# Order of the scores, the row maxima and what stands beside them in a step of TensorE

## The chip, the core and the metric

The kernel runs as one program on one core of a Trainium2 chip. The metric is the device time of an execution in microseconds; of the kernel before, three timed runs are given.

## What is computed

Eight sequences of 1024 tokens with 256 features go through two layers. Each layer normalises its input, and adds to it causal attention with 16 heads of 16 and a sparse expert network in which each token uses two of eight experts.

```
for x of 8 sequences:                        # (1024, 256)
    for layer in 0, 1:
        xn = layernorm(x)
        q, k, v = xn @ Wq.T, xn @ Wk.T, xn @ Wv.T
        o = softmax(causal(q k^T / 4)) v      # 16 heads of 16
        x = x + o @ Wo.T + experts(xn)
experts, layer 0: sum over 2 of 8 of score_e * (relu(xn @ W1[e] + b1[e]) @ W2[e] + b2[e])
experts, layer 1: sum over 2 of 8 of gate_e * (xn @ We[e] + be[e])
```

## The kernel before

A *run* is one sequence in one layer; there are 16. Runs are staggered on one long row of *steps*, written out by hand: each run has 48 steps of attention (a *unit*: one block of 128 keys for the four heads of a set, against up to 512 queries), and in the same steps TensorE does other runs' work. A table of step offsets (`XT`, `PROJ`, `VALUES`, `Y`, `OT`, `TURN`, ...) says when each of these is due. A *set* is four heads by 512 queries; it has 4 or 8 units. In the last four units of a set the scores get narrower (512, 384, 256, 128 columns), since queries ahead of the keys fall away.

All engines run their lists in order, and they meet through semaphores. `step(g)` of each engine writes the list. In TensorE's step, for j = 0 to 3, stand:

- `maxima` (M0 to M3, line 1160): bf16 scores with queries on the partitions, of another set, into the ring `pmx` of four banks. VectorE takes their row maxima (lines 875 and 879). In four steps of a group the products are 512 columns wide; in the steps on the diagonal they are 128, 256, 384 and 512 wide ("narrow maxima"), which is 32 of the 48 steps of a run;
- `scores` (S0 to S3, line 1147): bf16 scores of the unit with keys on the partitions, with the maxima folded in, into the ring `pst` of three banks. ScalarE makes the exponentials (line 722), one per head;
- beside the first member, `hidden` (H, line 1179), the first product of an expert tile of layer 0, which ScalarE reads at line 735;
- beside the third member, what the tables name: transposes of x (line 1216), `project` (line 1290, into `pmx`), `values` (line 1301), `project_output` (lines 1246 and 1249, into `pmx`);
- beside the fourth, `expert_out` (O, line 1194), which ScalarE copies at line 744.

Ahead of them a step may have `turn_tokens` (T, line 1168, read at line 727), and behind them the transposes of an ended set (line 1228), of the maxima (line 1222), and `attend` (A, line 1210) for the unit before. An expert tile starts every second step for 46 of 48 steps: in runs whose tiles are of layer 0, T and then H and then O stand in three steps that follow each other, so T and the O of the tile before share a step; with tiles of layer 1, T stands in odd steps and O in even ones. When a set ends, ScalarE copies its sums (`oraw`, line 751) between the first and the second exponential.

The rings give banks in TensorE's program order. The function `uses` counts them; `st` (line 1133) waits until the product three places earlier has been read, and `mx` until that four places earlier. GpSimd masks the block on the diagonal (line 621) once the fourth exponential is done, and then does its other work of the step, such as the last part of the split of a projection (line 627). VectorE splits the row maxima of a set in two instructions (lines 1042 and 1043).

Of the kernel before, what the change touches and what calls it, by code (L numbers as in the profile page):

```python
# [129 lines left out]
def unit(g):  # L130
    q, u = divmod(g, NU)
    return (q, u) if 0 <= q < NR else None
# [14 lines left out]
def tile_hidden(g):  # L147
    tile = tile_turned(g, 1)
    return tile if tile and layer(tile[0]) == 0 else None
# [32 lines left out]
def uses():  # L182

    mx, st = {}, {}
    for g in range(BEGIN, NR * NU + END - NU):
        if tile_turned(g):
            st["tokens", *tile_turned(g)] = len(st)
        work = maxima_at(g)
        turns = at_step(g, TURN)
        for j in range(GH):  # L190
            for q, n, k in work[j:j + 1]:
                mx["max", q, n, k] = len(mx)
            if j == 2:
                for (c, k), q in at_step(g, XT):
                    st["xT", q, c, k] = len(st)
                for (c, n), q in at_step(g, PROJ):
                    mx["proj", q, c, n] = len(mx)
                for t, q in at_step(g, VALUES):
                    st["v", q, t] = len(st)
                for b, q in at_step(g, Y):  # L200
                    mx["y", q, b] = len(mx)
            if j == 3 and tile_out(g):
                st["out", *tile_out(g)] = len(st)
            if unit(g):
                st["unit", *unit(g), j] = len(st)
            if j == 0 and tile_hidden(g):
                st["hidden", *tile_hidden(g)] = len(st)
        for q, n in set_ended(g):
            mx["set", q, n] = len(mx)
        for n, q in turns:  # L210
            mx["turn", q, n] = len(mx)
        for c, q in at_step(g, OT):
            for k in range(KD):
                st["oT", q, c, k] = len(st)
        for _, q in at_step(g, [GATE_ROWS]):
            mx["pos", q] = len(mx)
            mx["gateT", q] = len(mx)
        for _, q in at_step(g, [INVERSE]):
            mx["rows", q] = len(mx)
    return mx, st  # L220


MX, ST = uses()


def attention_moe_kernel(nc, A, out):
    ctx = ExitStack()
    with ctx:
# [462 lines left out]
        def _(act):  # L691
# [72 lines left out]
            def middle_parts(q, c, n):  # L764
                act.wait_ge(mx_read, mx_done("proj", q, c, n))
                act.activation(parts[:, n // 2, n % 2, 1], rest[:, n % 2], ACT.Copy).then_inc(mid_ready, 1)  # L766
# [20 lines left out]
            def step(g):  # L787
# [9 lines left out]
                    exponentials(*unit(g), 1)  # L797
                for (c, n), q in at_step(g - 1, PROJ):
                    middle_parts(q, c, n)
                for (c, k), q in at_step(g, XT):  # L800
                    take_x(q, c, k)
                for (c, n), q in at_step(g, PROJ):
# [1 line left out]
                for t, q in at_step(g, VALUES):  # L804
                    take_values(q, t)
                if unit(g):
                    exponentials(*unit(g), 2)
                if tile_out(g):
                    take_result(*tile_out(g))
                if unit(g):  # L810
                    exponentials(*unit(g), 3)
                for _, q in at_step(g, [GATES + 1]):
                    if layer(q) == 1:
                        act.wait_ge(logits_ready, q // 4 * 2 + q % 2 + 1)
# [311 lines left out]
        def _(pe):  # L1126
# [184 lines left out]
            def step(g):  # L1311
                work = maxima_at(g)
                if tile_turned(g):
                    turn_tokens(*tile_turned(g))
                for j in range(GH):
                    for piece in work[j:j + 1]:
                        maxima(*piece)
                    if j == 2:
# [7 lines left out]
                            project_output(q, b)  # L1326
                    if j == 3 and tile_out(g):
                        expert_out(*tile_out(g))
                    if unit(g):
                        scores(*unit(g), j)  # L1330
                    if j == 0 and tile_hidden(g):
                        hidden(*tile_hidden(g))
                for q, n in set_ended(g):
                    turn_set(q, n)
                for n, q in at_step(g, TURN):
# [58 lines left out]
```

## Time and profile before

| | us |
|---|---|
| three timed runs | 3098.23, 3103.86, 3106.82 (median 3103.86) |
| profiled execution | 3109.94 |
| its span from the first to the last instruction | 3108.2 |
| TensorE matmuls, weight loads busy | 2990.0, 1585.0 |
| VectorE, ScalarE, GpSimd busy | 2420.6, 1973.1, 1191.5 |

Matmuls overlap, so that the busy time of TensorE says little of what it could still take; the distance between two starts says how long one holds the next. In the rows, "k_first" and "k_second" are the two halves of the keys, `probs` the exponentials. A row of a timeline has the start in us from the span's start, the duration in us, the engine, the line, the operation, and what it writes and reads.

### The profile page before, as it was taken

Reading aid. Unit: us, or ns where it says so; the run is one execution under the profiler, and the core shown is the slowest. Engines: PE = TensorE matmul, PEld = TensorE weight load, DVE = VectorE, ACT = ScalarE, POOL = GpSimd, SP = SyncE. Lnnn points to the kernel's source line nnn. Section 1 sums busy time; section 2 is a strip of 40 time slices with the busy share of each in tenths; the row PEclk is TensorE's granted clock in tenths of the full one; section 3 lists DMA queues with packets and bytes.
Section 4 is the critical chain, followed back from the end, with each engine's and each line's share of the span. In section 5 each row is a group of like instructions: output and inputs, shape, how many; then the busy total and the mean of one; then the engine's idle time right before and its main releaser. Section 6 shows DMA issues by size and latency. Waiting matters only on the chain.

```text
span 3108.2 us, 62739 instructions
## 1 busy us (share of the span) xinstructions
PE 2990.0 (96%) x19312; PEld 1585.0 (51%) x19312; DVE 2420.6 (78%) x7517; ACT 1973.1 (63%) x4954; POOL 1191.5 (38%) x1424
## 2 busy tenths in 40 slices
PE   5899999999999999999999999999999999999998
PEld 3555555445455554545445555454545555545453
DVE  6677788887877778888777787878887777787884
ACT  2566666666666666666666666666666666666665
POOL 3225235252432524435252352534425244252533
PEclk8999999999999999999999999999999999999999
DMA  5677445364554645446364464635537455453542
GB/s 141 184 180 209 137 138 157 116 184 133 165 186 128 179 135 161 150 113 182 118 200 148 146 179 140 173 108 148 177 108 214 139 171 170 128 162 110 162 141 69
DMA packets 276876, 473.27 MB, mean 152 GB/s; under 512 B 52960, under 2 KB 185792, under 8 KB 274496
## 3 DMA queue, kind: packets, MB, share of 16 engines
q1 hardware_dynamic: 236928, 379.48, 40.5%
q0 software_dynamic: 29952, 81.83, 9.8%
q10 hardware_dynamic: 9664, 7.93, 0.9%
q8 instruction: 159, 2.61, 0.3%
q14 instruction: 173, 1.42, 0.2%
HBM read 344.19 MB, written 130.03 MB: 153 GB/s over the span
## 4 chain that ended last, share of the span: by engine, by line
PE 78%; DVE 10%; issue 4%; DMA 4%; ACT 3%; SPq 1%; POOL 1%; ACTq 0%; DVEq 0%; POOLq 0%
PE po L1210 16%; PE pmx L1160 14%; PE pst L1147 13%; PE pst L1194 9%; PE pmx L1290 5%; PE pst L1179 5%; PE pst L1301 4%; DVE pmx L879 3%; PE pmx L1249 3%; PE pst L1168 3%; DMA wt<-w_tiles 2%; PE pmx L1228 2%; PE pst L1216 2%; DVE rmax L875 1%; ACT probs L722 1%
## 5 line engine op out<-in xcount | busy, mean ns | idle before, releaser
L722 ACT ACTIVATE probs<-pst 128x512 f32<-128x512 f32 (+3 forms) x3072 | 1402.5, 497 | 413.6 <-PE pst L1147 409.6
L621 POOL TENSOR_SCALAR_AFFINE_SELECT probs<-probs 128x512 f32<-128x512 f32 x512 | 326.2, 637 | 1473.6 <-ACT probs L722 1472.5
L875 DVE TENSOR_REDUCE rmax<-pmx 128x1 f32<-128x512 f32 x1024 | 671.0, 682 | 133.0 <-PE pmx L1160 126.5
L1147 PE MATMUL pst<-qs,k_first 98*128 98x512 bf16 (+3 forms) x2048 | 689.2, 342 | 8.7 <-ACT probs L722 4.3
L1160 PE MATMUL pmx<-k_first,qs 96*128 96x512 bf16 (+2 forms) x2048 | 669.5, 343 | 14.3 <-DVE rmax L879 5.7
L879 DVE CUSTOM_DVE_ANT_0 pmx<-pmx,mask,rmax 128x128 f32<-128x128 f32 (+3 forms) x1024 | 534.5, 555 | 164.2 <-PE pmx L1160 154.3
L1210 PE MATMUL po<-probs,v 128*32 128x512 f32 (+3 forms) x6144 | 656.0, 499 | 4.2 <-POOL probs L621 4.2
L879 DVE CUSTOM_DVE_ANT_0 pmx<-pmx,mask 128x128 f32<-128x128 f32 (+3 forms) x1024 | 483.3, 509 | 138.0 <-PE pmx L1160 136.8
L594 POOL DMA_INDIRECT xg<-xn_rows,rows_of x368 | 357.9, 973 | 95.7 <-issue 50.8
L1160 PEld LDWEIGHTS pmx<-k_first,qs 96*128 96x128 bf16 x2048 | 198.8, 98 | 348.5 <-issue 123.7
L1160 PE MATMUL pmx<-k_second,qs 96*128 96x128 bf16 (+3 forms) x1024 | 304.9, 302 | 17.4 <-DVE otok L1016 8.7
L1147 PE MATMUL pst<-qs,k_second 98*128 98x512 bf16 (+3 forms) x1024 | 300.4, 301 | 3.0 <-ACT probs L722 2.2
L608 POOL DMA_INDIRECT yk<-y_slots,slot x256 | 245.1, 957 | 127.4 <-DVE x L1036 48.1
L1147 PEld LDWEIGHTS pst<-qs,k_first 98*128 98x128 bf16 x2048 | 199.6, 98 | 178.0 <-ACT probs L722 50.9
L879 DVE DVE_READ_ACCUMULATOR2_ANT rmax<- 128x1 f32 x2048 | 287.4, 140 | 0.0
L744 ACT ACTIVATE ys<-pst 128x256 f32<-128x256 f32 x368 | 142.9, 388 | 179.5 <-PE pst L1194 135.8
L1290 PE MATMUL pmx<-xnT,wqk 128*128 128x512 f32 x512 | 248.0, 607 | 7.4 <-DVE rmax L875 6.6
L1210 PEld LDWEIGHTS po<-probs,v 128*32 128x32 f32 x6144 | 121.2, 108 | 219.8 <-issue 171.9
L627 POOL TENSOR_TENSOR parts<-rest,parts 128x512 bf16<-128x512 f32 x128 | 148.8, 1163 | 191.9 <-ACT parts L766 191.9
L727 ACT ACTIVATE xgT<-pst 128x256 f32<-128x256 f32 x368 | 142.6, 387 | 118.8 <-PE pst L1168 116.3
L1179 PE MATMUL pst<-xgT,wt 128*128 128x128 f32 x1472 | 198.9, 279 | 19.7 <-DMA wt<-in_b 11.6
L1179 PEld LDWEIGHTS pst<-xgT,wt 128*128 128x128 f32 x1472 | 190.1, 194 | 36.2 <-DMA wt<-in_b 13.1
(143 smaller groups left out, 3514.3 us busy)
## 6 DMA issues: line engine op xcount, KB each, us to landing
wt<-w_tiles SPq DMA_DIRECT2D x161, 513.0 KB
qk_parts<-parts SPq DMA_DIRECT2D x256, 192.0 KB
y_slots<-ys SPq DMA_DIRECT2D x368, 128.0 KB
wt<-w_tiles SPq DMA_DIRECT2D x184, 256.0 KB
qs<-qk_parts SPq DMA_DIRECT2D x128, 192.0 KB
xn_rows<-xn SPq DMA_DIRECT2D x16, 1024.0 KB, 6.1
qs<-qk_parts SPq DMA_DIRECT2D x128, 128.0 KB
k_first<-qk_parts SPq DMA_DIRECT2D x64, 192.0 KB, 3.8
```

The costliest lines, as they stand in the source:

```text
L594: pool.indirect_dma_start(out=xg[:, m % XRING], out_offset=None, in_=xn_dram[q % 2], in_offset=bass.IndirectOffsetOnAxis(ap=rows_of[:, q % ...
L608: pool.indirect_dma_start(out=yk[:, m % GRING], out_offset=None, in_=y_dram[q % 2], in_offset=bass.IndirectOffsetOnAxis(ap=slot[:, q % 2, ...
L621: pool.affine_select(out=tri, in_=tri, compare_op=ALU.is_ge, fill=0.0, base=0, pattern=[[0, GH], [1, P]], channel_multiplier=-1).then_inc( ...
L722: act.activation(probs[:, u % 2, j, 0:w], ps[:, 0:w], ACT.Exp, scale=DH ** -0.5).then_inc(st_read, 1)
L875: dve.tensor_reduce(rmax0[:, col:col + 1], src, AX_X, ALU.max).then_inc(mx_read, 1)
L879: dve.tensor_tensor_reduce(out=src, in0=src, in1=mask[:, BANK - (b - a):BANK], op0=ALU.add, op1=ALU.max, scale=1.0, scalar=rmax0[:, col:co ...
L1147: pe.matmul(ps[:, 0:w], keys[0:SROWS, j, k % HT * P:(k % HT + 1) * P], qs[0:SROWS, set_no(q, n) % QRING, j, a:a + w], start=True, stop=Tru ...
L1160: pe.matmul(bk[:, 0:b - a], qs[0:STACK, set_no(q, n) % QRING, j, t % HT * P:(t % HT + 1) * P], keys[0:STACK, j, 0:b - a], start=True, stop ...
L1179: mm = pe.matmul(ps[:, j * P:(j + 1) * P], wt[:, m % WRING, a:a + P], xgT[:, m % 2, k], start=(k == 0), stop=(k == KD - 1))
L1194: mm = pe.matmul(ps[:, 0:D], src[:, m % 2, k], wt[:, m % WRING, a:a + D], start=(k == 0), stop=(k == KD - 1))
L1210: mm = pe.matmul(po[HS * j:HS * (j + 1), BANK - w:BANK], v[:, q % 2, k, col:col + HS], probs[:, u % 2, j, 0:w], start=(k == 0), stop=(u in ...
L1290: mm = pe.matmul(ps[:], wqk[l][:, m, k, tile * P:(tile + 1) * P], xnT[:, k, c * BANK:(c + 1) * BANK], start=(k == 0), stop=(k == KD - 1))
```

## The change

In TensorE's step the pair of a member is turned round: the scores (and, at the first member, `hidden`) come first, then the piece of maxima, then what stands beside the member. So the products beside the third member stand behind its scores, and `expert_out` stands behind all four scores. The counts of the rings follow. ScalarE takes the third exponential ahead of x, the projection's high part and the values, and the fourth ahead of the copy of `expert_out`. VectorE, GpSimd and the DMA lists are the same.

```diff
@@ uses(), and likewise step(g) of TensorE
         for j in range(GH):
+            if unit(g):
+                st["unit", *unit(g), j] = len(st)
+            if j == 0 and tile_hidden(g):
+                st["hidden", *tile_hidden(g)] = len(st)
             for q, n, k in work[j:j + 1]:
                 mx["max", q, n, k] = len(mx)
             if j == 2:
...
             if j == 3 and tile_out(g):
                 st["out", *tile_out(g)] = len(st)
-            if unit(g):
-                st["unit", *unit(g), j] = len(st)
-            if j == 0 and tile_hidden(g):
-                st["hidden", *tile_hidden(g)] = len(st)
@@ step(g) of ScalarE
                     middle_parts(q, c, n)
+                if unit(g):
+                    exponentials(*unit(g), 2)
                 for (c, k), q in at_step(g, XT):
                     take_x(q, c, k)
...
                 if unit(g):
-                    exponentials(*unit(g), 2)
+                    exponentials(*unit(g), 3)
                 if tile_out(g):
                     take_result(*tile_out(g))
-                if unit(g):
-                    exponentials(*unit(g), 3)
```

TensorE's list in a step with O (unit 34 of a run, expert tiles of layer 1), before:

```order
L1160 MATMUL pmx<-k_second,qs 128x128
L1147 MATMUL pst<-qs,k_first 128x512
L1160 MATMUL pmx<-k_second,qs 128x256
L1147 MATMUL pst<-qs,k_first 128x512
L1160 MATMUL pmx<-k_second,qs 128x384
L1147 MATMUL pst<-qs,k_first 128x512
L1160 MATMUL pmx<-k_second,qs 128x512
L1194 MATMUL pst<-wt,xgT 128x256 x2
L1147 MATMUL pst<-qs,k_first 128x512
L1210 MATMUL po<-probs,v 32x512 x4
```

and after the change:

```order
L1147 MATMUL pst<-qs,k_first 128x512
L1160 MATMUL pmx<-k_second,qs 128x128
L1147 MATMUL pst<-qs,k_first 128x512
L1160 MATMUL pmx<-k_second,qs 128x256
L1147 MATMUL pst<-qs,k_first 128x512
L1160 MATMUL pmx<-k_second,qs 128x384
L1147 MATMUL pst<-qs,k_first 128x512
L1160 MATMUL pmx<-k_second,qs 128x512
L1194 MATMUL pst<-wt,xgT 128x256 x2
L1210 MATMUL po<-probs,v 32x512 x4
```

L1147 are the scores, L1160 the maxima, L1194 is O and L1210 A. The four scores now stand with one M between two of them, and O stands ahead of A, behind the last M.

TensorE's list in a step with H (unit 34, tiles of layer 0), before:

```order
L1160 MATMUL pmx<-k_second,qs 128x128
L1147 MATMUL pst<-qs,k_first 128x512
L1179 MATMUL pst<-xgT,wt 128x128 x4
L1160 MATMUL pmx<-k_second,qs 128x256
L1147 MATMUL pst<-qs,k_first 128x512
L1160 MATMUL pmx<-k_second,qs 128x384
L1147 MATMUL pst<-qs,k_first 128x512
L1160 MATMUL pmx<-k_second,qs 128x512
L1147 MATMUL pst<-qs,k_first 128x512
L1210 MATMUL po<-probs,v 32x512 x4
```

and after:

```order
L1147 MATMUL pst<-qs,k_first 128x512
L1179 MATMUL pst<-xgT,wt 128x128 x4
L1160 MATMUL pmx<-k_second,qs 128x128
L1147 MATMUL pst<-qs,k_first 128x512
L1160 MATMUL pmx<-k_second,qs 128x256
L1147 MATMUL pst<-qs,k_first 128x512
L1160 MATMUL pmx<-k_second,qs 128x384
L1147 MATMUL pst<-qs,k_first 128x512
L1160 MATMUL pmx<-k_second,qs 128x512
L1210 MATMUL po<-probs,v 32x512 x4
```

H (L1179) keeps its place behind the first scores, but the first M now stands behind H; the last M stands behind the last scores.

ScalarE's list around the copy of an ended set's sums (L751), in a step with T, O and a projection's middle part (L766), before:

```order
L727 ACTIVATE xgT<-pst 128x256
L722 ACTIVATE probs<-pst 128x512
L751 ACTIVATE oraw<-po 128x512
L722 ACTIVATE probs<-pst 128x512
L766 ACTIVATE parts<-rest 128x512
L722 ACTIVATE probs<-pst 128x512
L744 ACTIVATE ys<-pst 128x256
```

and after:

```order
L727 ACTIVATE xgT<-pst 128x256
L722 ACTIVATE probs<-pst 128x512
L751 ACTIVATE oraw<-po 128x512
L722 ACTIVATE probs<-pst 128x512
L766 ACTIVATE parts<-rest 128x512
L722 ACTIVATE probs<-pst 128x512 x2
L744 ACTIVATE ys<-pst 128x256
```

The copy of O (L744) has moved from ahead of the fourth exponential to behind it.

## Rows read from the trace of the kernel before

**Rows 1.** The page: busy time, and the clock in 40 slices.

```profile
PE 2990.0 (96%) x19312; PEld 1585.0 (51%) x19312; DVE 2420.6 (78%) x7517; ACT 1973.1 (63%) x4954; POOL 1191.5 (38%) x1424
...
PEclk8999999999999999999999999999999999999999
```

**Rows 2.** Groups by form, TensorE: busy us, mean ns, idle us, releasers.

```profile
L1147 PE MATMUL pst<-qs,k_first 98*128 98x512 bf16 x1280 | 480.0, 382 | 4.6 <-ACT probs L722 3.4 <-ACT attn L785 0.3
```

**Rows 3.** The view of waits: us in total, times, longest us.

```profile
PEld pmx L1160 <- DVE rmax L879: 118.4, 200, 1.2
...
PEld pst L1147 <- ACT probs L722: 65.2, 181, 0.9
...
PEld pst L1194 <- ACT probs L722: 25.2, 73, 0.9
```

**Rows 4.** Timeline, TensorE, step with O: start, us, instruction.

```profile
1560.21 0.22 PE L1160 MATMUL pmx<-k_second,qs 96*128 96x128 bf16 x1
1560.27 0.38 PE L1147 MATMUL pst<-qs,k_first 98*128 98x512 bf16 x1
1560.48 0.27 PE L1160 MATMUL pmx<-k_second,qs 96*128 96x256 bf16 x1
...
1561.48 1.10 PE L1194 MATMUL pst<-wt,xgT 128*128 128x256 f32 x4
1562.42 0.38 PE L1147 MATMUL pst<-qs,k_first 98*128 98x512 bf16 x1
1562.73 0.64 PE L1210 MATMUL po<-probs,v 128*32 128x512 f32 x4
```

**Rows 5.** Timeline, ScalarE, same step.

```profile
1560.74 0.60 ACT L722 ACTIVATE probs<-pst 128x512 f32<-128x512 f32 x1 [0.61 <-PE pst L1147]
1561.24 0.59 ACT L722 ACTIVATE probs<-pst 128x512 f32<-128x512 f32 x1
```

**Rows 6.** Timeline, TensorE, step with T.

```profile
1563.73 0.44 PE L1168 MATMUL pst<-ident,xg 128*128 128x128 f32 x2
...
1565.52 0.64 PE L1210 MATMUL po<-probs,v 128*32 128x512 f32 x4
```

**Rows 7.** Timeline, ScalarE, same step.

```profile
1564.20 0.38 ACT L727 ACTIVATE xgT<-pst 128x256 f32<-128x256 f32 x1 [0.65 <-PE pst L1168]
1564.54 0.60 ACT L722 ACTIVATE probs<-pst 128x512 f32<-128x512 f32 x1
1565.04 0.59 ACT L722 ACTIVATE probs<-pst 128x512 f32<-128x512 f32 x1
```

**Rows 8.** Timeline, TensorE, step with H.

```profile
1198.56 0.22 PE L1160 MATMUL pmx<-k_second,qs 96*128 96x128 bf16 x1
...
1198.84 1.06 PE L1179 MATMUL pst<-xgT,wt 128*128 128x128 f32 x8
...
1200.99 0.64 PE L1210 MATMUL po<-probs,v 128*32 128x512 f32 x4
```

**Rows 9.** Timeline, ScalarE, same step.

```profile
1199.99 0.62 ACT L735 ACTIVATE hT<-pst,wt 128x128 f32<-128x128 f32 x2 [0.30 <-PE pst L1179]
```

**Rows 10.** Timeline, TensorE, step with T, O and a set's end.

```profile
1193.82 0.44 PE L1168 MATMUL pst<-ident,xg 128*128 128x128 f32 x2
...
1195.46 1.10 PE L1194 MATMUL pst<-wt,hT 128*128 128x256 f32 x4
...
1196.62 0.60 PE L1228 MATMUL pmx<-ident,oraw 128*128 128x128 f32 x4
```

**Rows 11.** Timeline, ScalarE, same step, second exponential.

```profile
1195.64 0.66 ACT L722 ACTIVATE probs<-pst 128x512 f32<-128x512 f32 x1
```

**Rows 12.** VectorE instructions of line 1043: ns min/median/max.

```profile
L1043 DVE SCALAR_TENSOR_TENSOR mparts<-rmax,mparts x128: 174/175/1719, 61.6 to 3061.5; 128x16 bf16<-128x16 f32 x128
```

**Rows 13.** Timeline, GpSimd, beside a long one of line 1043.

```profile
1052.82 1.15 POOL L627 TENSOR_TENSOR parts<-rest,parts 128x512 bf16<-128x512 f32 x1
```

**Rows 14.** Timeline, VectorE, the long one.

```profile
1052.30 1.71 DVE L1043 SCALAR_TENSOR_TENSOR mparts<-rmax,mparts 128x16 bf16<-128x16 f32 x1
```

More of the change, by code:

```diff
@@ L1315, in step @@
                 for j in range(GH):
+                    if unit(g):
+                        scores(*unit(g), j)
+                    if j == 0 and tile_hidden(g):
+                        hidden(*tile_hidden(g))
                     for piece in work[j:j + 1]:
@@ L1328, in step @@
                         expert_out(*tile_out(g))
[L1329 to L1332, printed above, removed]
                 for q, n in set_ended(g):
```

## The prediction

> **What bounds the kernel now.** I began with the page: the matmul side of TensorE is busy for 2990.0 of 3108.2 us and the clock row stands at 9 nearly everywhere, so every stage hangs on TensorE at its 2.4 GHz level [rows 1]. But busy time here is the sum of overlapping durations. By form, a 512-column score product lasts 382 ns [rows 2], while in a step two neighbours start 0.21 us apart (1560.27 and 1560.48 [rows 4]). So I read starts, not durations, and asked where one start lies further behind the last than the columns explain. The view of waits names the candidates [rows 3]: weight loads of the row maxima held by VectorE for 118.4 us, those of the scores held by ScalarE's exponentials for 65.2 us, those of the experts' last product for 25.2 us. (A weight load is where TensorE waits; not all of it reaches the matmuls.) TensorE takes its instructions in program order, so any such wait delays all that follows. The change moves the work that lies between such waits.
>
> The ring behind the score waits is `pst`, three banks. Write S0 to S3 for the scores of a step, M0 to M3 for the maxima, T for the token transposes, H for `hidden`, O for `expert_out`, A for `attend`. T, H, O, the scores, and also the transposes of x and the values (X below) go through the ring in program order, and each needs the product three places earlier to have been read by ScalarE. M, `project` and the output projection use the other ring, `pmx`, that VectorE empties.
>
> **The change, part by part.** No product is added or removed. Per step, each M moves behind the S of its number, H moves ahead of M0, products beside the third member move behind S2, and O moves behind S3 and M3. Total streaming is the same; fixed gaps at A should be too. What changes is the distance between scores, and whom O waits for.
>
> *Step with O and no T.* Before: S0 starts at 1560.27, O at 1561.48, S3 at 1562.42, A at 1562.73, 2.52 us after the step's M0 [rows 4]. ScalarE ends the first exponential at 60.74 + 0.60 = 61.34, which is S0 + 1.07, and the second at 61.83, S0 + 1.56 [rows 5]. O stood 0.14 behind the first one's end, since its fp32 weight load comes after the wait. I use 0.05 for a score after such an end and 0.14 for O. After: S0 at 0, M0 0.21, S1 0.27, M1 0.48, S2 0.59, M2 0.81, and S3 would be due at 0.97 (narrow maxima stream 0.05, 0.11, 0.16 and 0.21 us). Its ring place is S0's, free at 1.12. Then M3, and O would start at 1.55 but now needs S1's place: 1.56 + 0.14 = 1.70. O to the next product took 0.94, A stands 0.09 behind: 2.73. Loss 0.21 us.
>
> *Step with T, no O.* Before 1.79 us from T to A [rows 6]. Tokens are read at 64.59, T + 0.86; exponentials end at T + 1.41 and T + 1.90 [rows 7]. After: S2, due at T + 0.87, needs the tokens' place, 0.91; S3, due at 1.29, needs S0's, 1.46; M3 to 1.89; A at 1.98. Loss 0.19.
>
> *Step with T and O.* Before, from the same rows, O at 1.41 + 0.14 = 1.55, A at 1.55 + 0.94 + 0.31 = 2.80. After, O at 1.90 + 0.14 = 2.04, A at 3.07. Loss 0.27.
>
> *Step with H.* Before 2.43 from M0 to A [rows 8]. `hT` is read at 1199.99 + 0.62 = 1200.61, H + 1.77 [rows 9]. H now starts at S0 + 0.21, S3 needs its place: 0.21 + 1.77 + 0.05 = 2.03 (due at 1.84), M3, A at 2.03 + 0.21 + 0.21 + 0.09 = 2.54. Loss 0.11, with roundings 0.12.
>
> *Step with T, O and the end of a set.* ScalarE copies `oraw` between the first and the second exponential, so the second ends at 1195.64 + 0.66 = 1196.30, T + 2.48 [rows 11]. Before, O needed only the first and ran under this copy, from T + 1.64; the transposes of the set start at T + 2.80 [rows 10]. After, O waits until 2.62 and the set until 3.56. Loss 0.76; I take 0.7, since the earlier fourth score of the step before lightens ScalarE's backlog.
>
> Where the maxima of a step are all 512 wide, S3 falls due at 1.29 (no T) and 1.56 (T), behind 1.12 and 1.46: no loss, except where the scores are 128 wide (S2 due at 0.81 against 0.91: 0.1). With `project` or the output projection behind S2, S3 is late anyway: no loss, and its exponential no longer queues behind the copy of the projection. Where x's transposes or the values stand there, they now wait for the first exponential themselves: about 0.16.
>
> *Counts.* A run has 48 steps; in half of the 16 runs the expert tiles are of layer 0 (with H), in half of layer 1. Steps of one pair of runs with narrow maxima: O alone with wide scores 4 x 0.21, one more 0.1; T alone 2 x 0.19 and, with narrower scores, 6 x 0.15; T and O 2 x 0.27 and 5 x 0.15; H 6 x 0.12; set with T and O 3 x 0.7, and one held by VectorE anyway 0.15; set with T 3 x 0.16; X beside the third member 12 x 0.16; wide maxima under 128-wide scores 6 x 0.1. Sum 9.5 us, times 8: 76 us. The 0.15 and 0.16 are estimates from the four steps above with shorter exponentials.
>
> *What comes back.* M waits: each S now stands ahead of the M that waits, but the M that starts VectorE's chain is later by an S as well. I take nothing. VectorE's queue, though, is filled by blocked instructions: the second part of the maxima's split takes 175 ns in the median and up to 1719 ns [rows 12], and a long one ends at 1052.30 + 1.71 = 1054.01, just behind GpSimd's subtraction, 1052.82 + 1.15 = 1053.97 [rows 13, 14]. That GpSimd work stands behind the causal mask, which waits for the fourth exponential; S3 now comes ahead of O and the chain moves forward by up to 1 us, out of the split's way. The bound: one long split in each of 16 runs, 1719 - 175 ns each, 25 us of VectorE, of which TensorE can get back only what it waits for afterwards. I take 10; the ends are 0 and 25.
>
> The Trainium skill (SBUF — State Buffer, Who interferes with whom) says that a VectorE instruction with two SBUF inputs blocks against a GpSimd instruction that reads SBUF, whichever came first holding the ports to its end. The split has two SBUF inputs, and the two ends agree within 0.04 us. By the rule the chain only has to shift, and may as well fall on another VectorE instruction; by the row I count the relief.
>
> Sum: 3109.94 (the profiled execution) + 76 - 10 = 3176. The median of the three runs, 3103.86, lies 6 lower: 3170 us, +2.1%.
>
> The Trainium skill (Perfetto Trace Analysis, Optimization Strategy) says that a gap that repeats on the engine that should be saturated can mean too few buffers for the next tile. Here the repeat is O's 0.14 us behind an exponential. By the rule, spacing ring users apart helps, and the change does the reverse.
>
> **The rivals.** *Absorbed.* TensorE's new waits fall where it would have waited for VectorE a step later; the 118.4 us of held weight loads speak for it, against it that in the steps worked out VectorE has no part. If nine tenths vanish: +8, about 3112. *Faster.* The place is the first steps behind a projection. If the whole bound of 25 us reaches TensorE and ScalarE's shorter queue there gives 5 more, 30 us come back; it decides if ScalarE's freed places are seen some 0.2 us earlier than I read them, which takes the losses away in all but the set steps (3 x 0.7 x 8 = 17). Then 3104 + 17 - 30 = 3091. Against it: O stood 0.14 behind the exponential, so the places are felt. *Deeper.* In H steps M0 now comes behind H, so VectorE idles under H and gets four maxima in a row; if that adds 0.3 us to each of the 8 x 23 steps with H, +55: 3225.
>
> **How the numbers follow.** Forecast 0.62, absorbed 0.13, faster 0.11, deeper 0.14. Its own range is 3145 to 3190 (losses a third smaller, or no relief). For 8 in 10 I reach down half way to the absorbed case and up part of the way to the deeper one: 3118 to 3198. What a measurement of this kernel can tell from no change is 0.3%, 9 us. Absorbed straddles that: 0.06 of it same, 0.07 slower; slower in all 0.83, same 0.06, faster 0.11.
>
> **What would show it.** After, in a step with O, A should start 2.7 us after S0, with O close behind the second exponential; T to A 1.98; the set step's O at T + 2.6. Waits of L1147 and L1194 for L722 should at least double, those of L1160 for VectorE stay or shrink, and the long splits at step 0 be gone. I am wrong if the fourth score starts 0.97 after the first in such a step, or if DVE waits grow instead.

## The result, and the profile after

| | us |
|---|---|
| before, four runs beside the changed kernel | 3105.34 (3098.23 to 3107.44) |
| changed, four runs | 3187.64 (3184.88 to 3188.56) |
| ratio | 1.0262, interval 1.0245 to 1.0280 |
| span of the profiled execution | 3108.2 before, 3186.8 after |

The change makes the kernel 82 us slower; between the two profiled spans it is 78.6. The page of the kernel after, with its busy times and the clock:

```profile
PE 3050.2 (96%) x19312; PEld 1547.8 (49%) x19312; DVE 2417.3 (76%) x7517; ACT 1962.4 (62%) x4954; POOL 1193.2 (37%) x1424
...
PEclk8999999999999999999999999999999999999999
```

The counts are those of [rows 1], and so is the clock row: TensorE is granted its 2.4 GHz level nearly all the time in both (the granted clock is 0.991 of full speed in the mean before and 0.993 after; 0.002 of 3108 us is 6 us, an estimate of the most that this gave the changed kernel). Its busy share is 96% as before, with 2.6% more time. The share says nothing here; a matmul that waits under the end of the one before it looks busy. The view of waits after, total us, times, longest:

```profile
PEld pst L1147 <- ACT probs L722: 199.8, 401, 1.0
...
PEld pst L1147 <- ACT ys L744: 97.3, 116, 0.8
POOL yk L608 <- DVE x L1036: 82.5, 63, 3.5
PEld pst L1147 <- ACT xgT L727: 81.9, 310, 0.4
...
PEld pmx L1160 <- DVE rmax L879: 64.7, 134, 1.0
...
PEld pst L1194 <- ACT probs L722: 47.4, 88, 0.9
```

Against [rows 3], the scores' waits for the exponentials tripled (65.2 to 199.8 us), those of O nearly doubled (25.2 to 47.4), and those of the maxima for VectorE halved (118.4 to 64.7). TensorE has traded waits for VectorE for waits for ScalarE. (A wait in this view need not cost time. The 97.3 us of the scores for `ys`, which had no such row before, stand behind A: in unit 26 S0's weight load starts 0.99 us behind A's start, where M0's did before.) The steps show what the waits are worth.

*Step with O, no T.* TensorE's timeline, the same step as [rows 4]:

```profile
1597.68 0.38 PE L1147 MATMUL pst<-qs,k_first 98*128 98x512 bf16 x1
...
1598.80 0.39 PE L1147 MATMUL pst<-qs,k_first 98*128 98x512 bf16 x1
1599.03 0.38 PE L1160 MATMUL pmx<-k_second,qs 96*128 96x512 bf16 x1
1599.38 1.10 PE L1194 MATMUL pst<-wt,xgT 128*128 128x256 f32 x4
1600.41 0.64 PE L1210 MATMUL po<-probs,v 128*32 128x512 f32 x4
```

S3 starts 1.12 us after S0, O 1.70, A 2.73: the three numbers worked out before, to the hundredth. Before, the step took 2.52, so it costs 0.21.

*Step with T.* TensorE, the same step as [rows 6]: T, S2, S3, A. Then ScalarE's reading of the tokens and its first exponentials:

```profile
1601.41 0.44 PE L1168 MATMUL pst<-ident,xg 128*128 128x128 f32 x2
...
1602.32 0.39 PE L1147 MATMUL pst<-qs,k_first 98*128 98x512 bf16 x1
...
1602.81 0.39 PE L1147 MATMUL pst<-qs,k_first 98*128 98x512 bf16 x1
...
1603.35 0.64 PE L1210 MATMUL po<-probs,v 128*32 128x512 f32 x4
```

```profile
1601.88 0.38 ACT L727 ACTIVATE xgT<-pst 128x256 f32<-128x256 f32 x1 [0.92 <-PE pst L1168]
1602.16 1.57 ACT L722 ACTIVATE probs<-pst 128x512 f32<-128x512 f32 x3
```

S2 starts at T + 0.91 as worked out, but S3 at T + 1.40 (I had 1.46) and A at T + 1.94 (1.98). ScalarE's first exponential starts at T + 0.75; in [rows 7] it was T + 0.81. The reason stands in the order of the instructions: S0 used to follow M0 and now comes ahead of it, 0.06 us earlier. I had carried the old exponential times over unchanged.

*Step with H.* TensorE, the same step as [rows 8]: S0, H, S3, A; then ScalarE's `hT`:

```profile
1227.88 0.38 PE L1147 MATMUL pst<-qs,k_first 98*128 98x512 bf16 x1
1228.10 1.05 PE L1179 MATMUL pst<-xgT,wt 128*128 128x128 f32 x8
...
1229.93 0.39 PE L1147 MATMUL pst<-qs,k_first 98*128 98x512 bf16 x1
...
1230.47 0.64 PE L1210 MATMUL po<-probs,v 128*32 128x512 f32 x4
```

```profile
1229.25 0.62 ACT L735 ACTIVATE hT<-pst,wt 128x128 f32<-128x128 f32 x2 [0.30 <-PE pst L1179]
```

`hT` is read at 1229.87, H + 1.77 as in [rows 9]; S3 follows 0.06 later and A 0.54 after that. The step takes 2.59 instead of 2.43.

*Step with T, O and the end of a set.* TensorE, the same step as [rows 10], then ScalarE, where the copy of `oraw` (L751) stands ahead of the second exponential as in [rows 11]:

```profile
1222.53 0.44 PE L1168 MATMUL pst<-ident,xg 128*128 128x128 f32 x2
...
1225.00 1.10 PE L1194 MATMUL pst<-wt,hT 128*128 128x256 f32 x4 [0.46 <-ACT probs L722]
1225.94 0.60 PE L1228 MATMUL pmx<-ident,oraw 128*128 128x128 f32 x4
```

```profile
1223.77 0.59 ACT L751 ACTIVATE oraw<-po 128x512 f32<-128x512 f32 x1
1224.25 0.61 ACT L722 ACTIVATE probs<-pst 128x512 f32<-128x512 f32 x1
```

The second exponential ends at 1224.86, T + 2.33; O starts at T + 2.47 and the set at T + 3.41, against T + 1.64 and T + 2.80 before.

Taken over the whole program, from the start of one A to that of the next in each of the 768 steps, the difference of the two traces falls on the kinds of step as follows (sums over the 16 runs):

| kind of step | worked out | measured |
|---|---|---|
| O alone, narrow maxima | 6.7 | 6.8 |
| T alone | 3.0 | 2.4 |
| T alone, narrower scores | 7.2 | 6.2 |
| T and O | 4.3 | 3.2 |
| T and O, narrower scores | 6.0 | 5.4 |
| H | 5.8 | 7.3 |
| set with T and O, three steps | 16.8 | 13.4 |
| set with T and O, unit 25 and the narrow one | 1.2 | 6.7 |
| set with T | 3.8 | -1.0 |
| x's transposes or values beside the third member | 15.4 | 17.5 |
| 128-wide scores under wide maxima | 4.8 | 4.7 |
| sum of these | 75.0 | 72.7 |
| units 0 and 40, which gained | 0 | -9.4 |
| units 4, 5, 31 and 32, which lost | 0 | 13.4 |
| unit 26 | 0 | -3.1 |
| all other steps | 0 | 5.2 |
| relief of VectorE's queue, somewhere | -10 | none found |

(The prediction's 76 has one more O step at 0.1, and roundings; the measured column sums to 78.8 up to roundings, the spans differ by 78.6.) So most losses stand where they were placed, and what stayed away is the relief. The two sums, 75.0 and 72.7, agree better than their rows, which miss by -4.8 to +5.5 us: that part of the agreement is luck.

One more wait differs between the two traces, and the prediction has no term for it. In steps with H, TensorE waits until the expert's weights have landed; what L1179 waited for, us in total and times, first before, then after:

```profile
  DMA wt<-w_tiles: 20.4, 21
```

```profile
  DMA wt<-w_tiles: 9.6, 17
```

The view adds the idle time of the weight loads to that of the matmuls, so that the time won is about half of the difference, some 5 us. In the traces of the twelve versions the figure is anything from 4.6 to 31.2. The waits fall mostly in units 0, 4 and 40 with tiles of layer 0, and one trace of each kernel doesn't show whether their shrinking here belongs to the new order.

### The profile page after: what moved, and what is told of

Its sections match the earlier page's. It is cut to its first block, busy times and chain, and to the rows that moved or that the text cites. A ratio compares the mean times of both kernels' runs of the same rounds, so it can differ in the third digit from the quotient of the medians.

```text
span 3186.8 us, 62739 instructions
## 1 busy us (share of the span) xinstructions
PE 3050.2 (96%) x19312; PEld 1547.8 (49%) x19312; DVE 2417.3 (76%) x7517; ACT 1962.4 (62%) x4954; POOL 1193.2 (37%) x1424
## 3 DMA queue, kind: packets, MB, share of 16 engines
q14 instruction: 173, 1.42, 0.2%
## 4 chain that ended last, share of the span: by engine, by line
PE 77%; DVE 10%; ACT 5%; issue 4%; DMA 2%; SPq 1%; POOL 1%; ACTq 0%; DVEq 0%; POOLq 0%
PE po L1210 16%; PE pst L1147 14%; PE pmx L1160 12%; PE pst L1194 9%; PE pst L1179 5%; PE pmx L1290 5%; PE pst L1301 4%; PE pmx L1249 4%; DVE pmx L879 3%; PE pst L1168 3%; PE pmx L1228 2%; ACT probs L722 2%; DMA wt<-w_tiles 1%; PE pst L1216 1%; DVE rmax L875 1%
## 5 line engine op out<-in xcount | busy, mean ns | idle before, releaser
L722 ACT ACTIVATE probs<-pst 128x512 f32<-128x512 f32 (+3 forms) x3072 | 1358.1, 497 | 448.4 <-PE pst L1147 433.9
L621 POOL TENSOR_SCALAR_AFFINE_SELECT probs<-probs 128x512 f32<-128x512 f32 x512 | 328.4, 641 | 1485.7 <-ACT probs L722 1484.6
L1160 PE MATMUL pmx<-k_first,qs 96*128 96x512 bf16 (+2 forms) x2048 | 670.3, 342 | 16.0 <-DVE rmax L879 4.5
L1147 PE MATMUL pst<-qs,k_first 98*128 98x512 bf16 (+3 forms) x2048 | 665.2, 344 | 18.2 <-ACT probs L722 6.1
L1210 PE MATMUL po<-probs,v 128*32 128x512 f32 (+3 forms) x6144 | 655.0, 498 | 3.3 <-POOL probs L621 3.3
L1147 PEld LDWEIGHTS pst<-qs,k_first 98*128 98x128 bf16 x2048 | 198.5, 97 | 384.5 <-ACT probs L722 119.3
L1160 PE MATMUL pmx<-k_second,qs 96*128 96x128 bf16 (+3 forms) x1024 | 304.4, 301 | 14.6 <-DVE otok L1016 7.9
L1147 PE MATMUL pst<-qs,k_second 98*128 98x512 bf16 (+3 forms) x1024 | 293.4, 303 | 8.4 <-ACT xgT L727 5.7
L608 POOL DMA_INDIRECT yk<-y_slots,slot x256 | 245.6, 960 | 147.2 <-DVE x L1036 82.5
L1160 PEld LDWEIGHTS pmx<-k_first,qs 96*128 96x128 bf16 x2048 | 201.6, 99 | 167.8 <-DVE rmax L879 44.8
L744 ACT ACTIVATE ys<-pst 128x256 f32<-128x256 f32 x368 | 141.9, 386 | 186.7 <-PE pst L1194 186.3
L1210 PEld LDWEIGHTS po<-probs,v 128*32 128x32 f32 x6144 | 121.0, 108 | 229.5 <-issue 149.9
L1179 PE MATMUL pst<-xgT,wt 128*128 128x128 f32 x1472 | 197.7, 277 | 13.4 <-DMA wt<-in_b 10.0
L1194 PE MATMUL pst<-wt,hT 128*128 128x256 f32 x736 | 195.1, 387 | 14.1 <-ACT probs L722 14.0
```

The costliest lines, as they stand in the source:

```text
L608: pool.indirect_dma_start(out=yk[:, m % GRING], out_offset=None, in_=y_dram[q % 2], in_offset=bass.IndirectOffsetOnAxis(ap=slot[:, q % 2, ...
L621: pool.affine_select(out=tri, in_=tri, compare_op=ALU.is_ge, fill=0.0, base=0, pattern=[[0, GH], [1, P]], channel_multiplier=-1).then_inc( ...
L722: act.activation(probs[:, u % 2, j, 0:w], ps[:, 0:w], ACT.Exp, scale=DH ** -0.5).then_inc(st_read, 1)
L1147: pe.matmul(ps[:, 0:w], keys[0:SROWS, j, k % HT * P:(k % HT + 1) * P], qs[0:SROWS, set_no(q, n) % QRING, j, a:a + w], start=True, stop=Tru ...
L1160: pe.matmul(bk[:, 0:b - a], qs[0:STACK, set_no(q, n) % QRING, j, t % HT * P:(t % HT + 1) * P], keys[0:STACK, j, 0:b - a], start=True, stop ...
L1179: mm = pe.matmul(ps[:, j * P:(j + 1) * P], wt[:, m % WRING, a:a + P], xgT[:, m % 2, k], start=(k == 0), stop=(k == KD - 1))
```

## The experiments

My theory: each product of the ring `pst` needs the place three products earlier, ScalarE frees it, and the new order brings these neighbours closer (scores 0.27 to 0.33 us apart instead of with O between them) or puts a long reader between. A rival: the loss comes from the other ring, since M0 now comes later and VectorE is fed later. Every experiment is one edit of a copy of one of the two kernels. Kernels with fewer ring waits, the parts alone, and the reader's place and duration tell the theories apart.

### A fourth bank for the scores, on either order

```diff
-MXRING, STRING = 4, 3
+MXRING, STRING = 3, 4
```

On the kernel before:

> The order of before, with four banks in the ring of scores (pst) and three in the ring of maxima (pmx). It is the base for the next run. The smaller pmx ring lets VectorE hold TensorE more often: 3105 to 3200 us. Ring theory: waits of L1147 and L1194 for L722 all but vanish. VectorE theory: the same, so this run alone does not tell them apart.

On the changed kernel:

> The order of after, with four banks for pst and three for pmx. Ring theory (the loss of 82 us is the wait for the place three products back in pst): with a place four back, S3 waits for nothing of its own step and expert_out needs the first exponential only, so this run lies within 15 us of before_pst4. VectorE theory (the loss comes because the maxima stand later and VectorE is fed late): the loss stays or grows with the smaller pmx ring, 60 us or more over before_pst4.

Measured: 3241.32 (ratio 1.0432, interval 1.0411 to 1.0454) and 3257.13 (1.0485, 1.0458 to 1.0512). The change costs 16 us with four banks for the scores, 82 with three. The granted clock of the profiled executions is 0.982 and 0.986 here, and 0.991 and 0.993 with three banks, so the 16 may be too low by up to 13 us (0.004 of 3250, an estimate). The waits of the two, first the kernel before with four banks:

```profile
PEld pmx L1160 <- DVE rmax L879: 185.8, 352, 1.3
```

then the changed kernel with four:

```profile
PEld pmx L1160 <- DVE rmax L879: 113.7, 272, 0.8
...
PEld pst L1147 <- ACT probs L722: 96.9, 122, 0.8
```

Before, the scores' waits for exponentials fell as expected, from 65.2 us to 11.3. After, 96.9 of 199.8 are left, which I had not expected; in the steps looked at they don't reach the matmuls. The step with O of the changed kernel with four banks, TensorE:

```profile
1642.67 0.38 PE L1147 MATMUL pst<-qs,k_first 98*128 98x512 bf16 x1
...
1643.65 0.38 PE L1147 MATMUL pst<-qs,k_first 98*128 98x512 bf16 x1
...
1644.09 1.03 PE L1194 MATMUL pst<-wt,xgT 128*128 128x256 f32 x4
1645.05 0.64 PE L1210 MATMUL po<-probs,v 128*32 128x512 f32 x4
```

S3 starts at S0 + 0.98 and O at S0 + 1.42, both where they fall due without a wait. Units 34 to 36 and 42 to 44 lose 0.00 to 0.04 us each. That is the ring theory's forecast for these steps. As a measure of the whole it is weaker, because the bank is taken from the maxima: that costs 134 us on the kernel before (of which the lower clock, 0.009 of 3245 us, may be up to 29, an estimate), and TensorE's waits for VectorE could hide ring losses elsewhere. So the same question was put again without touching the rings (the halved exponentials below).

The Trainium skill (Perfetto Trace Analysis, Matmuls) says that independent groups of matmuls should rotate through different banks so that one's evacuation overlaps the next one's products. Both kernels do that. The runs add that it is the distance between users that counts: the same three banks cost 0 or 0.21 us a step, by the order alone.

### Only O moved behind the fourth scores

On the kernel before; TensorE, the count of the ring and ScalarE's list alike:

```diff
-                    if j == 3 and tile_out(g):
-                        expert_out(*tile_out(g))
                     if unit(g):
                         scores(*unit(g), j)
+                    if j == 3 and tile_out(g):
+                        expert_out(*tile_out(g))
```

> Of the change only one part: expert_out stands behind the fourth scores (M3 S3 O), on ScalarE its copy behind the fourth exponential. Ring theory: O needs the second exponential, in steps with an ended set the one behind the copy of oraw. Worked out from the starts: 0.25 us in each narrow step with O, 0.6 in each with T, O and a set's end, about 50 us in all, 3155 (3140 to 3170), nearly all of it in steps with O. VectorE theory: nothing, 3105, since no maxima move against the streaming ahead of them.

Measured: 3180.86 (1.0246, 1.0226 to 1.0266), 26 above what I expected. TensorE in the step with O:

```profile
1592.92 0.38 PE L1147 MATMUL pst<-qs,k_first 98*128 98x512 bf16 x1
...
1594.07 0.38 PE L1147 MATMUL pst<-qs,k_first 98*128 98x512 bf16 x1
1594.62 1.10 PE L1194 MATMUL pst<-wt,xgT 128*128 128x256 f32 x4 [0.18 <-ACT probs L722]
1595.65 0.64 PE L1210 MATMUL po<-probs,v 128*32 128x512 f32 x4
```

O again at S0 + 1.70, held by the second exponential. The step costs 0.27 here (M0 stands ahead of S0), and the set steps with T and O 0.67 to 0.76; I had expected 0.25 and 0.6. What I missed: in steps with wide maxima O falls due at about S0 + 1.50 and waits as well, 0.20 to 0.25 us, and steps that also carry x's products or the values lose 0.21 to 0.68. In the whole change M3 stands between S3 and O and fills just this wait, so such a wide step (units 20, 28 and 29) loses 0.00 to 0.05.

### Only the products beside the third member moved behind its scores

```diff
                     if j == 2:
+                        if unit(g):
+                            scores(*unit(g), j)
                         for (c, k), q in at_step(g, XT):
...
-                    if unit(g):
+                    if unit(g) and j != 2:
                         scores(*unit(g), j)
```

> Of the change only one part: the third scores stand ahead of the products beside the third member (M2 S2 X M3 S3). Ring theory: transposes of x and values now wait for the first exponential, 0.2 us in each of 12 such narrow steps of a pair of runs (+19 us), while steps with a projection gain what they gained after the change (about 9 us): 3115 (3105 to 3125). Rival (ScalarE's shorter queue behind a projection is worth more than that): below 3100.

Measured: 3147.46 (1.0147, 1.0123 to 1.0171), 32 above the forecast. The reason is the same: here x's transposes and the values follow S2 with no maxima between, so that the wide steps lose 0.17 to 0.44 too, 20 us in sum, and the narrow ones 0.11 to 0.44, except unit 17, which loses nothing. Unit 26 loses 4.8 us in sum, which was not traced. The gains that I had looked for in units 0, 30, 32 and 40 are 0.11 to 0.25 in a step, each with tiles of one of the two layers only.

### Only the other pairs turned

The first, second and fourth pair turned; the third member, x's products and O as before.

```diff
-                    for piece in work[j:j + 1]:
+                    for piece in work[j:j + 1] if j == 2 else []:
                         maxima(*piece)
...
                         hidden(*tile_hidden(g))
+                    for piece in work[j:j + 1] if j != 2 else []:
+                        maxima(*piece)
```

> Of the change only the turned pairs: scores (and hidden) ahead of the maxima at members 1, 2 and 4; at the third member and for expert_out the order is that of before (M2 X S2, then O, S3, M3). Ring theory: M3 no longer fills the time in which S3 waits for its place, so narrow steps with T or H lose 0.15 and those with O 0.15 to 0.2; some 40 us, 3148 (3135 to 3160). If the loss of the change came from O and from the products beside the third member alone, this kernel is as fast as before.

Measured: 3148.62 (1.0142, 1.0125 to 1.0160). In units 34 to 44 a step with H loses 0.16, with T 0.15, with T and O 0.16, with O 0.16, as expected. The total is met in part by luck: unit 26 gains 9.1 us in sum, and units 1, 30 and 31 lose 6.0, 4.6 and 4.1, none of them in the forecast. With x's products moved alone 40 us, O alone 74 and this 43, the parts sum to 157 us and the whole costs 82. I read this as parts that share one wait: a step pays the time by which its worst product comes too early for its place, not each product's; a maxima piece between two users delays the second and shrinks its wait.

### Only the first pair turned

This puts M0 behind H, where it comes 0.9 us later in a step with H, and leaves the scores' distances nearly alone.

```diff
-                    for piece in work[j:j + 1]:
+                    for piece in work[j:j + 1] if j else []:
                         maxima(*piece)
...
                         hidden(*tile_hidden(g))
+                    for piece in work[j:j + 1] if j == 0 else []:
+                        maxima(*piece)
```

> Only the first pair is turned: S0, hidden, M0, then all as before. Ring theory: the distance from S0 and from H to the later users of the ring does not shrink, so 3107 within 10 us. VectorE theory (M0 behind hidden feeds VectorE late and all maxima come in a row): each of the 184 steps with hidden loses 0.1 to 0.3 us, 3125 to 3160.

Measured: 3113.47 (1.0030, 1.0016 to 1.0044; six runs of the version against nine of the kernel before, 3105.7). Outside unit 0 a step with H changes by -0.06 to +0.03 in the median, so the rival falls as the main cause. It is not empty, though: unit 31 loses 0.55 us with tiles of layer 0, unit 29 0.29, unit 5 0.36 to 0.40, and other steps give much of it back (units 6, 10 and 40 gain 2.6 to 3.1 in sum each). Unit 0 loses 6.9 us in sum, but there H waits for its weights: the figure for that wait, counted as above, is 31.2 us in this trace against 20.4, so the 7.8 us of this run can't be put down to VectorE alone. Of the 13.4 us that the changed kernel loses in units 4, 5, 31 and 32, late feeding fits the 4.2 of unit 31 with tiles of layer 0, 0.54 to 0.55 a step in both, and some of unit 5. Units 4 and 32 lose 5.7 us there with tiles of layer 1 and nothing here, so their cause stays open.

### Exponentials of half the columns, on either order

ScalarE exponentiates the left half of a member's columns only; the right half of `probs` is set to zero once, so the queries of that half get zero sums. Everything else, the rings included, is as it was.

```diff
+            pool.memset(probs[:], 0.0)
...
-                act.activation(probs[:, u % 2, j, 0:w], ps[:, 0:w], ACT.Exp, scale=DH ** -0.5).then_inc(st_read, 1)
+                act.activation(probs[:, u % 2, j, 0:w // 2], ps[:, 0:w // 2], ACT.Exp, scale=DH ** -0.5).then_inc(st_read, 1)
```

On the kernel before:

> The kernel before, with exponentials of the left half of the columns only (the right half of probs cleared once, then stale): the base for the same edit of the kernel after, which measured 3124.02. Ring theory with ScalarE's pace as the cause: before gains little by it, since it has few score waits, 3085 to 3105, and the difference between the two orders is 20 to 35 us instead of 82. If ScalarE's pace is not the cause, the order costs 82 us here too: about 3045.

On the changed kernel:

> The kernel after, with exponentials of the left half of the columns only (the right half of probs is cleared once at the start and then stale). ScalarE gives back a place in pst about 0.25 us sooner. Ring theory, with ScalarE's pace as the cause: what is left of the loss are steps with hidden (0.16 us) and part of the set steps; 10 to 35 us over the kernel before in full, less what the shorter ScalarE work saves elsewhere: 3110 to 3140. If the order costs by itself (weight loads, VectorE), it stays near 3188, 3165 or more.

Measured: 3081.93 (0.9933, 0.9913 to 0.9953) and 3124.02 (1.0063, 1.0043 to 1.0083). The change costs 42 us here instead of 82 (39 if each is set against its own runs of the kernel before); I had expected 20 to 35. TensorE in the step with O of the changed order (the scores are line 1148 there, O is 1195, A 1211):

```profile
1567.53 0.38 PE L1148 MATMUL pst<-qs,k_first 98*128 98x512 bf16 x1
...
1568.52 0.38 PE L1148 MATMUL pst<-qs,k_first 98*128 98x512 bf16 x1
...
1568.95 1.03 PE L1195 MATMUL pst<-wt,xgT 128*128 128x256 f32 x4
1569.91 0.64 PE L1211 MATMUL po<-probs,v 128*32 128x512 f32 x4
```

The 0.21 us are gone: S3 at S0 + 0.99, O at S0 + 1.42, A at S0 + 2.38, and the two orders differ by 0.00 in these steps. Steps with T, or T and O, keep 0.04 where the scores are 512 wide and 0.15 to 0.17 where they are narrower; these narrower steps, 9.5 us in sum, were not in what I had expected to stay. A step with H keeps its whole 0.16, as it should, since there S3 waits for `hT`, which the edit doesn't shorten. The same step's rows, H, its reading by ScalarE and S3:

```profile
1207.15 1.05 PE L1180 MATMUL pst<-xgT,wt 128*128 128x128 f32 x8
...
1208.99 0.39 PE L1148 MATMUL pst<-qs,k_first 98*128 98x512 bf16 x1
```

```profile
1208.31 0.62 ACT L736 ACTIVATE hT<-pst,wt 128x128 f32<-128x128 f32 x2 [0.51 <-PE pst L1180]
```

`hT` ends at 1208.93, H + 1.78, and S3 follows 0.06 later. The set steps 9, 25 and 33 keep 0.39 to 0.46 (the copy of `oraw` isn't halved), unit 41 0.15, x's steps up to 0.38. So in the steps worked out, with O and with H, the loss follows the duration of whatever holds the place.

### The copy of a set's sums behind the second exponential

If the set steps lose because O waits for an exponential queued behind the copy of `oraw`, the copy can step back. On the changed kernel, ScalarE's list:

```diff
-                for q, n in set_ended(g):
+                for q, n in set_ended(g) if not tile_out(g) else []:
                     take_set(q, n)
...
+                for q, n in set_ended(g) if tile_out(g) else []:
+                    take_set(q, n)
```

> The kernel after, but in steps that end a set and have expert_out, ScalarE copies oraw behind the second exponential instead of ahead of it. Ring theory: O then waits as in any other step with T and O, the four narrow ones of a run with tiles of layer 0 lose 0.2 instead of 0.6 us: 12 us less than after, 3175 (3168 to 3182). If the wait in these steps is something else (weights, the set itself): 3188 as after.

Measured: 3175.45 (1.0229, 1.0211 to 1.0246). TensorE in the same set step (the lines stand two lower; O is 1196, the set's transposes 1230):

```profile
1216.30 0.44 PE L1170 MATMUL pst<-ident,xg 128*128 128x128 f32 x2
...
1218.29 1.10 PE L1196 MATMUL pst<-wt,hT 128*128 128x256 f32 x4
1219.23 0.60 PE L1230 MATMUL pmx<-ident,oraw 128*128 128x128 f32 x4
```

O at T + 1.99 instead of 2.47. Units 9, 25, 33 and 41 with tiles of layer 0 lose 0.49 less each, which is one exponential's turn on ScalarE. That shows the mechanism of this term by itself. It is worth its 0.49 in three of the four only: unit 26, behind unit 25, takes 0.49 more, and the two together last 8.41 us in both versions (7.44 to 8.53 before the change). There M3 waits for VectorE's normalising of the set (`otok`). Its weight load in unit 26, first in the changed kernel, then with the late copy (the same lines two lower):

```profile
988.21 0.10 PEld L1160 LDWEIGHTS pmx<-k_second,qs 96*128 96x128 bf16 x1 [0.64 <-DVE otok L1016]
```

```profile
984.78 0.10 PEld L1162 LDWEIGHTS pmx<-k_second,qs 96*128 96x128 bf16 x1 [1.13 <-DVE otok L1018]
```

The wait for VectorE is longer by the 0.49 that O no longer waits. Units 9, 33 and 41 give 11.3 us together. My forecast of 12 was four sets at 0.4, so the agreement in the total is in part luck.

### The same move on the kernel before

There the copy stands in the way of a different product only where x's transposes share the step.

```diff
-                for q, n in set_ended(g):
+                copy_late = tile_out(g) or at_step(g, XT)
+                for q, n in set_ended(g) if not copy_late else []:
                     take_set(q, n)
...
+                for q, n in set_ended(g) if copy_late else []:
+                    take_set(q, n)
```

> The kernel before, with the copy of an ended set's sums behind the second exponential, in steps that also have expert_out or a transpose of x. There the fourth product of the ring waits for the second exponential. Ring theory: step 17 of a run gains 0.5 us (tiles of layer 0) and 0.2 (layer 1), the other sets with O nothing to 0.1: 5 to 8 us in all, 3099. Rival: the transposes of the set, which need the copy, come later by the same time: no change.

Measured: 3099.00 (12 runs, 3092.19 to 3102.76) against 3102.38 (17 runs), 0.9984, interval 0.9975 to 0.9994. Unit 17 gains 0.49 us with tiles of layer 0 and 0.17 with layer 1, in sum 5.1 us; no other kind of step changes by more than 0.04 in the median. Of the versions that compute the whole result it is the fastest, 0.16% below the kernel before by the ratio of the runs, and the only gain found.

## Why the prediction came out as it did

*The direction, and the mechanism.* Right. The ring's places were the main cost, shown three ways: by a fourth bank and by shorter exponentials, each of which takes the loss out of the steps with O, and by the late copy, which takes 0.49 us out of each set step with T and O. The forecast 3170 lies 18 below 3187.64, inside its range. Of the 18, 10 are the relief below and 1.5 the median of the kernel before (3105.34, not 3103.86); nearly 3 are the 78.8 us of the steps against 76, and 4 the 82.3 us between the medians against 78.6 between the spans.

*The step that failed is the relief of 10 us.* I had argued that S3 ahead of O lets GpSimd's mask start earlier and moves its work out of the way of VectorE's split. Both halves can be read in the trace after. First the split (ns min/median/max):

```profile
L1043 DVE SCALAR_TENSOR_TENSOR mparts<-rmax,mparts x128: 174/176/1726, 61.6 to 3140.1; 128x16 bf16<-128x16 f32 x128
```

The long ones are still there: over their median the 128 instructions take 20.0 us more, before 20.8; over 1 us long are 13, before 12. Next GpSimd and VectorE at such a place, after:

```profile
1075.26 0.95 POOL L608 DMA_INDIRECT yk<-y_slots,slot  x1 [1.03 <-PE pst L1194]
1076.21 0.64 POOL L621 TENSOR_SCALAR_AFFINE_SELECT probs<-probs 128x512 f32<-128x512 f32 x1
1076.82 1.16 POOL L627 TENSOR_TENSOR parts<-rest,parts 128x512 bf16<-128x512 f32 x1
```

```profile
1076.30 1.72 DVE L1043 SCALAR_TENSOR_TENSOR mparts<-rmax,mparts 128x16 bf16<-128x16 f32 x1
```

Ahead of the mask (L621) stands the issue of a gather (L608). It stood there before too, two rows ahead of [rows 13] in the same view, and I had passed over it:

```profile
1051.26 0.94 POOL L608 DMA_INDIRECT yk<-y_slots,slot  x1 [0.76 <-PE pst L1147]
```

GpSimd takes its queue in order, and the mask starts as the gather's issue ends: at 1052.22 behind 1051.26 + 0.94 = 1052.20 before, at 1076.21 behind 1075.26 + 0.95 = 1076.21 after, and within 0.02 us of it at each of the 15 places where one run's units follow another's, in both traces. The fourth exponential did come earlier. The one that the mask needs ended at 1051.54 before, 0.66 ahead of the gather's end, and at 1074.55 after, 1.66 ahead. The mask did not follow it: counted from the start of unit 0's first product it runs from 0.77 to 1.41 us before and from 0.76 to 1.40 after, the subtraction from 1.37 to 2.52 and from 1.37 to 2.53. The gather itself needs VectorE. Here it starts 0.75 us behind the end of VectorE's L1036 in both traces (1050.03 + 0.48 before, 1074.03 + 0.48 after); by the code it waits for that instruction, and what fills the 0.75 is not shown. (The releaser in the rows' brackets is inferred; the product of `pst` that the code waits for had been done for long.) Over the whole program its waits for VectorE are 48.1 us before and 82.5 after. So the premise that the fourth exponential sets the start of GpSimd's work was wrong.

The Trainium skill (SBUF — State Buffer, Who interferes with whom) has VectorE's second input share ports with GpSimd, held as a lock. The trace agrees with it again: 1.72 us instead of 0.175, ending at 1078.02, where GpSimd's subtraction ends at 1077.98. By the rule the chain only had to shift; it did not shift.

*Sizes.* The narrow step with O came out exactly (0.21). T alone was 0.19 and measured 0.15, T with O 0.27 and 0.21: the missing 0.04 to 0.06 is M0's stream, which no longer stands ahead of S0. The same 0.06 explains why "set with T" was not +0.16 but -0.06: there the set's transposes waited for the copy of `oraw` anyway, and the copy comes 0.06 earlier. H was 0.12 and measured 0.16, half in S3's start, half in A's distance behind S3. The set steps with T and O were 0.7 and measured 0.56 to 0.61; of the 0.15 against the worked-out 0.76, 0.10 is the second exponential's earlier start (T + 1.72, not 1.82) and 0.05 its shorter duration (0.61, not 0.66).

*What I had counted at little or nothing.* For the set steps with T and O beyond three I had taken only 0.15 in one, since I saw VectorE hold it anyway; unit 25 lost 0.61 in each run with tiles of layer 0, 4.9 us in all. But it has to be taken together with unit 26, where 1.3 us of it come back, and the late copy shows that O's wait in unit 25 costs the two nothing in sum, since VectorE holds M3 in unit 26. So VectorE does hold this place, one step later than I had looked, and what the two lose, 3.6 us, has another cause, not traced (with only x's products moved the two lose 4.9). Of the 9.4 us that units 0 and 40 gained, 3.6 are in steps with tiles of layer 1, where M3 waits for VectorE, before and after, and the scores and their exponentials now go ahead of it; I had taken nothing for that. The other 5.7 are in steps with tiles of layer 0, where H also waits for its weights, and they can't be told from that wait. These gains and unit 26 about pay for the losses of units 4, 5, 31 and 32. The 5.2 us scattered over all other steps were not traced further.

*The rivals.* Absorbed falls as a whole: the steps' losses sum to 72.7 of 75. In units 25 and 26 it is what happened. Deeper is there only in a few steps (13.4 us where it would have needed 55), and the steps with H themselves lose nothing by it. Faster had 25 of its 30 us in the same relief that failed.

*What was to be seen.* A at S0 + 2.73, T to A 1.94 (said: 1.98), the set step's O at T + 2.47 (2.6), the waits of O 1.9 times (at least double), those of the maxima smaller: as said or near. The long splits at step 0 were to be gone, and they are not.

## What to carry to other kernels

In a ring of buffers whose users are of several kinds, write down for each product when it falls due and when the place that many products earlier is read. In the steps worked out here the order cost the largest of these differences and not their sum, and the long O between two scores paid for the short ring. What is won in one step can be lost in the next, where another engine holds (units 25 and 26), so add up over several steps. Parts of such a change must not be added up (157 us apart, 82 together), and one part alone can cost nearly as much as the whole (O, 74). Before counting on an engine's work to move earlier, read what stands ahead of it in that engine's own queue.

## What the runs showed of the hardware that was not expected

- The distance between a reader's end and the next user's start repeats closely: a bf16 score product starts 0.05 to 0.06 us behind the end of the ScalarE instruction that frees its place (1598.80 behind 1598.15 + 0.60, the first of four exponentials), an fp32 product with its own fp32 weights 0.14 (O at 1225.00 in the set step, behind 1224.25 + 0.61 = 1224.86; and [rows 4, 5]).
- Exponentials of 128x512 from the product banks last 0.59 to 0.61 us but start 0.48 to 0.49 apart (four in 2.06, from 1598.15 in the step with O after the change), so a queue of them frees a place about each 0.49 us; moving one instruction past another saves 0.49 and not 0.60.
- A bank is worth more to the maxima than to the scores: taking the fourth from the maxima and giving it to the scores costs 134 us on the kernel before, while the scores' waits for exponentials only fall from 65.2 to 11.3 in weight loads [rows 3].
- The busy share of matmuls stood at 96% with and without 82 us of added waits.
